# Folding token tiles on GpSimd ahead of a sum over all tokens, and a later, closer row of linear-attention steps

## The reference

```
xn = layernorm(x);  x = x + attention0(xn) + experts0(xn)     # softmax attention, top-2 experts
xn = layernorm(x);  x = x + attention1(xn) + experts1(xn)     # linear "flow" attention, top-4 experts
```

```
k_sum = k.sum(tokens);  sink_incoming   = 1 / sum((q + eps) * (k_sum + eps))
q_sum = q.sum(tokens);  source_outgoing = 1 / sum((k + eps) * (q_sum + eps))
k_so_sum = (k * source_outgoing).sum(tokens);  conserved_sink   = sum((q + eps) * (k_so_sum + eps)) + eps
q_si_sum = (q * sink_incoming).sum(tokens);    conserved_source = clip(sum((k + eps) * (q_si_sum + eps)) + eps, -1, 1)
out = ((q * sink_incoming) @ (k.T @ (v * softmax(conserved_source) * n))) * sigmoid(conserved_sink)
out = out @ proj_w.T + proj_b
```

## Time and profile before

| | us |
|---|---|
| median of 3 runs | 2818.09 |
| lowest and highest run | 2817.61, 2819.32 |
| the profiled execution | 2820.42 |
| its span | 2818.7 |
| PE busy | 2497.2 |
| DVE busy | 2185.9 |
| ACT busy | 1441.5 |
| POOL busy | 719.1 |

### The profile page before, as it was taken

One profiled execution on the slowest core, in us unless ns is written; L12 is line 12 of the kernel. 1 busy time (PEld: TensorE's weight loads), 2 busy tenths in 40 slices (PEclk: granted clock), 3 DMA queues, 4 the chain that ended last, 5 costly groups with the idle time before them and its releaser, 6 DMA issues.

```text
span 2818.7 us, 67301 instructions
## 1 busy us (share of the span) xinstructions
PE 2497.2 (89%) x26720; PEld 1807.0 (64%) x26720; DVE 2185.9 (78%) x3781; ACT 1441.5 (51%) x2616; POOL 719.1 (26%) x593
## 2 busy tenths in 40 slices
PE   4988989889898898988989889899898998989989
PEld 2766657675566665666667666576665766667656
DVE  4958878589786897777977779767797687985878
ACT  2746237563375534665246642566435573365723
POOL 1220342204322042220522215122151121520225
PEclk8999999999999999999999999999999999999999
DMA  6110211102111021110201112011120101201012
GB/s 224 39 37 4 87 49 39 38 2 98 38 39 38 2 102 35 39 38 25 82 31 42 35 39 75 24 46 31 47 71 26 44 27 54 68 27 47 19 63 65
DMA packets 93370, 136.25 MB, mean 48 GB/s; under 512 B 10111, under 2 KB 55240, under 8 KB 92552
## 3 DMA queue, kind: packets, MB, share of 16 engines
q1 hardware_dynamic: 84872, 115.16, 12.5%
q0 software_dynamic: 8192, 16.79, 2.0%
HBM read 101.31 MB, written 30.61 MB: 47 GB/s over the span
## 4 chain that ended last, share of the span: by engine, by line
PE 62%; DVE 19%; issue 11%; ACT 6%; POOL 2%; DVEq 0%; ACTq 0%; POOLq 0%
PE ps L1475 10%; PE ps L1343 8%; PE ps L1511 7%; PE ps L1417 6%; PE ps L1496 5%; DVE neg_max L1028 5%; PE ps L1548 4%; PE ps L1350 4%; PE ps L1439 3%; DVE probsT L1036 3%; ACT probs L701 2%; PE ps L1364 2%; PE ps L1317 2%; DVE ffn L1163 1%; PE ps L1428 1%
## 5 line engine op out<-in xcount | busy, mean ns | idle before, releaser
L1028 DVE TENSOR_REDUCE neg_max<-ps 128x1 f32<-128x1024 f32 x512 | 623.2, 1217 | 48.6 <-PE ps L1475 38.9
L701 ACT ACTIVATE probs<-ps,neg_max 128x1024 f32<-128x1024 f32 x512 | 571.6, 1117 | 156.3 <-DVE neg_max L1028 154.5
L1475 PE MATMUL ps<-keys,q_parts 64*128 64x512 f32 x3072 | 520.2, 445 | 82.8 <-ACT probs L701 57.0
L1343 PE MATMUL ps<-q_parts,w_split 128*128 128x512 f32 x1536 | 458.5, 435 | 42.6 <-DVE ffn L1146 24.0
L1496 PEld LDWEIGHTS ps<-ident,probs 64*128 64x128 f32 x8192 | 347.2, 143 | 96.4 <-ACT probs L701 17.3
L1343 PEld LDWEIGHTS ps<-q_parts,w_split 128*128 128x128 f32 x1536 | 284.7, 192 | 191.9 <-DVE ffn L1146 87.2
L1475 PEld LDWEIGHTS ps<-keys,q_parts 64*128 64x128 f32 x3072 | 264.1, 196 | 220.4 <-ACT probs L701 109.2
L600 POOL TENSOR_TENSOR probs<-ffn,q_parts 128x512 f32<-128x512 f32 x208 | 294.7, 1418 | 429.3 <-DVE ffn L1163 291.9
L757 ACT ACTIVATE ffn<-ffn 128x512 f32<-128x512 f32 x256 | 160.6, 630 | 468.8 <-DVE ffn L1146 468.4
L1036 DVE COPY probsT<-ps 128x512 f32<-128x512 f32 x512 | 348.6, 681 | 23.6 <-PE ps L1496 23.6
L1496 PE MATMUL ps<-ident,probs 64*128 64x64 f32 x8192 | 350.1, 227 | 16.4 <-ACT probsT L683 16.2
(11 more groups left out here) (213 smaller groups left out, 3297.0 us busy)
## 6 DMA issues: line engine op xcount, KB each, us to landing
w_split<-w_parts SPq DMA_DIRECT2D x132, 256.0 KB, 2.6
q_parts<-gate_rows SPq DMA_DIRECT2D x64, 512.0 KB, 4.0
y_rows<-probs SPq DMA_DIRECT2D x40, 256.0 KB, 2.2
x_in<-in_x SPq DMA_DIRECT2D x9, 512.0 KB, 4.3
w_parts<-q_parts SPq DMA_DIRECT2D x2, 2048.0 KB, 13.7
out<-x_mid SPq DMA_DIRECT2D x8, 512.0 KB, 3.2
ffn<-in_gate_up SPq DMA_DIRECT2D x1, 2048.0 KB, 8.9
probsT<-in_gate_up SPq DMA_DIRECT2D x1, 2048.0 KB, 13.1
```

The source lines that it names most:

```text
L701: nc.scalar.activation(probs[:, t % 3, :], banks(2 * (t % 2)), ACT.Exp, bias=neg_max[:, t % 4:t % 4 + 1], accum_out=row_sum[:, g % 2, t % ...
L1028: nc.vector.tensor_reduce(neg_max[:, t % 4:t % 4 + 1], banks(2 * (t % 2)), X, ALU.max, negate=True).then_inc(max_ready.sem, 1)
L1343: mm = nc.tensor.matmul(ps[:, bank, :], w_split[:, f % CHUNK_SLOTS, h, k * P:(k + 1) * P], tokens[:, half], start=(part == 0), stop=(part ...
L1475: mm = nc.tensor.matmul(ps[:, 2 * (t % 2) + c, :], q_parts[rows, j, q, n * P:(n + 1) * P], keys[rows, k, :], start=(part == 0), stop=(part ...
```

## The change

The sums over all tokens are made in two parts. POOL first adds token tiles 0 to 3 to tiles 4 to 7 (one instruction, 128x1024), and then the first two of these four to the other two (one instruction, 128x512). The two tiles that are left are summed by PE with two matmuls in place of eight. The tile `fold` takes the room of `v_comp`, which isn't in use at that point. `FLOW_HALVES` gives the units behind whose product POOL does the folds, 2 and 12. PE's sums wait for the fold (`folded`). All later steps of the linear attention get a higher unit number: the first sums move from unit 4 to 6, the second from 12 to 15, the values from 16 to 19, KV from 20 to 22, the output from 22 to 24, the heads from 25 to 26 and the projection from 28 to 29. The projection thus moves by one unit and the second sums by three, so that the steps between them stand closer together.

```diff
--- before.py
+++ after.py
@@ -51,7 +51,7 @@
 NORM_STATS = 8
 NORM_VAR = 13
 NORM_APPLY = 17
-NEXT_TRANSPOSE = 15
+NEXT_TRANSPOSE = 18
 
 
 H1, D1 = 16, 8
@@ -73,18 +73,19 @@
 
 FLOW_SIGMOID = 2
 SIGMOID_UNIT = 3
-FLOW_SUMS = 4
-
-FLOW_WEIGHTS = (4, 5, 6, 7, 8, 9)
+FLOW_SUMS = 6
+FLOW_HALVES = (2, 12)
+
+FLOW_WEIGHTS = (6, 7, 8, 9, 10, 11)
 FLOW_BIAS = 22
-FLOW_SUMS2 = 12
-FLOW_CONSERVED = (11, 12, 13, 14)
-FLOW_ALLOC = 15
-FLOW_VALUES = 16
-FLOW_KV = 20
-FLOW_OUT = 22
-FLOW_HEADS = 25
-FLOW_PROJ = 28
+FLOW_SUMS2 = 15
+FLOW_CONSERVED = (14, 15, 16, 17)
+FLOW_ALLOC = 18
+FLOW_VALUES = 19
+FLOW_KV = 22
+FLOW_OUT = 24
+FLOW_HEADS = 26
+FLOW_PROJ = 29
 
 DOWN_LAG = 4
 
@@ -197,6 +198,7 @@
         weighted = room[:, 3 * SEQ:5 * SEQ].rearrange("p (n c) -> p n c", n=NT)
         tmp = room[:, 5 * SEQ:6 * SEQ].rearrange("p (n c) -> p n c", n=NT)
         v_comp = room[:, 6 * SEQ:7 * SEQ].rearrange("p (n c) -> p n c", n=NT)
+        fold = room[:, 6 * SEQ:7 * SEQ].rearrange("p (n c) -> p n c", n=4)
 
         xT = [xT_first[:, :], room[:, 7 * SEQ:8 * SEQ]]
         q_normT = room[:, 7 * SEQ:8 * SEQ]
@@ -418,6 +420,7 @@
         sig_tanh = signal("sig_tanh", 1)
         qk_ready = signal("qk_ready", 1)
         sums_mm = signal("sums_mm", 2)
+        folded = signal("folded", 4)
         sums2_taken = signal("sums2_taken", 1)
         inv_flow_ready = signal("inv_flow_ready", 1)
         weighted_q = signal("weighted_q", 1)
@@ -601,6 +604,21 @@
                                             gate_bc[:, e % GATE_SLOTS, c * BANK:(c + 1) * BANK], ALU.mult
                                             ).then_inc(h_ready.sem, 1)
 
+                    if u in FLOW_HALVES:
+                        i = FLOW_HALVES.index(u)
+                        if i == 0:
+                            pool.wait_ge(qk_ready.sem, qk_ready.at(b, 1))
+                            x = qkv[:, :, 0:2 * D]
+                        else:
+
+                            pool.wait_ge(sums_mm.sem, sums_mm.at(b, 1))
+                            pool.wait_ge(weighted_q.sem, weighted_q.at(b, 1))
+                            pool.wait_ge(weighted_k.sem, weighted_k.at(b, 1))
+                            x = weighted
+                        nc.gpsimd.tensor_tensor(fold, x[:, 0:4, :], x[:, 4:8, :], ALU.add).then_inc(folded.sem, 1)
+                        pool.wait_ge(folded.sem, folded.at(b, 2 * i + 1))
+                        nc.gpsimd.tensor_tensor(fold[:, 0:2, :], fold[:, 0:2, :], fold[:, 2:4, :], ALU.add
+                                                ).then_inc(folded.sem, 1)
                     if u == FLOW_WEIGHTS[4]:
                         pool.wait_ge(inv_flow_ready.sem, inv_flow_ready.at(b, 1))
                         nc.gpsimd.tensor_tensor(heads(weighted[:, :, D:2 * D]), heads(flow_k),
@@ -1602,17 +1620,16 @@
                 def flow_step(u):
 
                     if u == FLOW_SUMS:
-                        pe.wait_ge(qk_ready.sem, qk_ready.at(b, 1))
-                        for n in range(NT):
-                            mm = nc.tensor.matmul(ps[:, 6, 0:2 * D], ones, qkv[:, n, 0:2 * D], start=(n == 0),
-                                                  stop=(n == NT - 1))
+                        pe.wait_ge(folded.sem, folded.at(b, 2))
+                        for n in range(2):
+                            mm = nc.tensor.matmul(ps[:, 6, 0:2 * D], ones, fold[:, n, :], start=(n == 0), stop=(n == 1))
                         mm.then_inc(sums_mm.sem, 1)
                     if u == FLOW_SUMS2:
                         pe.wait_ge(weighted_q.sem, weighted_q.at(b, 1))
                         pe.wait_ge(weighted_k.sem, weighted_k.at(b, 1))
-                        for n in range(NT):
-                            mm = nc.tensor.matmul(ps[:, 7, 0:2 * D], ones, weighted[:, n, :], start=(n == 0),
-                                                  stop=(n == NT - 1))
+                        pe.wait_ge(folded.sem, folded.at(b, 4))
+                        for n in range(2):
+                            mm = nc.tensor.matmul(ps[:, 7, 0:2 * D], ones, fold[:, n, :], start=(n == 0), stop=(n == 1))
                         mm.then_inc(sums_mm.sem, 1)
                     if u in (FLOW_SUMS2, FLOW_SUMS2 + 1):
                         c = u - FLOW_SUMS2
```

## The result

The changed kernel takes 2851.66 us (median of 4 runs, 2850.34 to 2855.58). In the same comparison the kernel before has 2817.85 us (4 runs, 2813.91 to 2819.32). The ratio is 1.0129, with a 95% interval from 1.0114 to 1.0144 (the quotient of the two medians is 1.0120). By the medians the change makes the kernel 34 us slower. The forecast was 2845 us, in a range from 2812 to 2856.

The account below looks back on a forecast made before the run. PE bounds units without a linear-attention step, DVE those with a weights or conserved step. Lost time of 3.6 us per sequence gives 8 x 3.6 = 29 us, taken as 27: 2818.1 + 27 = 2845 us, range 2812 to 2856.

Parts of the forecast that it names:

- PE's saved passes gain nothing: At both sums: 43 us less PE work over 8 sequences, the largest possible gain; at the second, DVE covers the saving.
- The fold's own price: On POOL, per sum: first add 2.35 us, second 1.28 us, about 3.7 us with its wait.
- DVE's products are held: Beside POOL's work: 2.1 us lost at the first fold, then about 1.1 and 0.1 us for units 4 and 5.
- sentence on two operands: A DVE instruction with two SBUF operands and a POOL instruction don't run together, so each fold stops the product beside it.
- The waits of PE: PE stalls 1.5 us at the first sums, 4 us at the second and 2.1 us before the KV matmuls.
- DVE's wait before the second sums: DVE waits 2.3 us before taking the second sums, whose inputs from the second fold are late.
- The sum: Per sequence the last down matmuls come 3.6 us later; 8 x 3.6 = 29 us, taken as 27 us.
- Its own signs: Short sums after 4 us idle; DVE idle 2 us; DVE products over 1.2 us; KV wait; POOL add 2.0 to 2.4.
- only a part of it: Rival, 20%: the wait before KV falls away or folds come between DVE's products; 1.5 us per sequence, 2830 us.
- Nothing in sum: Rival, 10%: folds and DVE's products run side by side; the stage ends within 0.1 us of before, 2818 us.
- Faster: Rival, 15%: DVE's product precedes the first fold, second fold ends before PE reaches the sums; 1.9 us won per sequence, 2803 us.
- Worse: Rival, 10%: POOL's delayed products meet DVE's in each unit, 0.5 us each over three more units; 2858 us.

Follow-up runs that it names:

- e9: Changed kernel with second sums and all steps behind them two units later, then KV, output and heads one more; 2814.61 us, ratio 0.9995.
- e11: Changed kernel without folds, eight matmuls for both sums, and KV, output, heads and projection one unit later; 2812.80 us, ratio 0.9984.
- e1: Changed kernel with its new unit numbers but no folds, both sums by eight matmuls on PE; 2825.73 us, ratio 1.0030.
- e5: Changed kernel with only the first fold, second sums by PE's eight matmuls again; 2824.66 us, ratio 1.0030.
- e4: Changed kernel with eight more matmuls on PE, result overwritten, ahead of its wait for the second fold; 2845.80 us (three runs), ratio 1.0100.
- e6: Changed kernel with only the second fold, first sums by PE's eight matmuls again; 2848.97 us, ratio 1.0105.
- e7: Changed kernel with the second sums and all steps behind them two units later, fold still behind unit 12; 2827.68 us, ratio 1.0033.
- e2: Against e1, POOL also does two folds of q and k tiles that nobody waits for or reads; 2840.69 us, ratio 1.0084.

## Why the prediction was right, step by step

- **PE's saved passes gain nothing: right.** The page shows 40.6 us less of PE (43 forecast), and e9 against e11 shows that of two folds 0.1 us per sequence reaches the end even where neither the second fold nor the values are waited for. From the sigmoid step to the first sums DVE has no idle time in the changed kernel, so its chain is the bound there.
- **The fold's own price: right.** 2.39 us for the first add where DVE didn't hold it (2.35 taken from the row of another one), 5.72 us from the sending of unit 12's product to the end of the second add (5.4 to 5.8 by the working).
- **DVE's products are held: right in place and size.** 2.80 - 0.68 = 2.1 us at the first fold, and 1.0 at the next product (1.1). The rows agree with what the prediction took from the Trainium skill (GPSIMD Engine Reference, 8. Key points): each of these products ends 0.55 us behind the POOL instruction that it met. But two SBUF operands are not the whole condition. The sigmoid step has one, keeps its 1.21 us, and POOL's product beside it takes 2.21 in place of 1.27. The prediction put such a row (996.57) under its sentence on two operands, which it doesn't fit. Also, e1 and e5 show that the holds at the first fold cost nothing in sum, since they take the place of the time that DVE otherwise waits for the eight matmuls. I had put the 3.5 us of lateness at the first sums under the heading of the fold. It is there in e1 without any fold (11.96 us), and belongs to the steps.
- **The waits of PE: right.** 1.3 us at the first sums (1.5 forecast), 3.96 at the second (4), 1.90 before KV (2.1). The rest from KV on is 25.96 us (25.9).
- **DVE's wait before the second sums: mis-sized.** 3.35 us in place of 2.3. Of the missing 1.05 us the slow clock in the sums themselves has 0.92 (2.05 - 1.13), and the same clock makes unit 16's matmuls late: 1.76 us more idle on DVE. I had costed the wait at its length alone and put the clock behind it at nothing. e4 puts the clock's part at 2.0 us in the third sequence and 1.6 on average.
- **The sum:** 3.6 us per sequence by the working, 5.2 measured in the stage (41.4 / 8). Some 1.4 us per sequence are missing outside the stage in the profiled execution, and 34 us in the medians are 4.2 per sequence. The forecast of 27 us was a fifth too small, by the term for the clock: the 1.6 us that the stage is over the working are what e4 gives back in it.
- **Its own signs:** of the five things it named three are there: short sums with 4 us of idle time before the second group, DVE products over 1.2 us beside each first add, and the wait before KV. Two are off in size, both at the second fold: DVE idles 3.35 us, not about 2, and the first add takes 2.80 us, outside 2.0 to 2.4. And the stretch from POOL's first product (992.73 before, 998.55 now) to the last group of down matmuls is 5.7 us longer, where the prediction called itself wrong outside 2.5 to 4.5. So the places and the order of the waits were right, and the size inside the stage was not. That the median, 2851.66 us, still lies just inside the forecast's own range of 2838 to 2852 is in part luck: the medians are 34 us apart, the stages of the profiles 41.
- **Shares:** of the 5.6 us of the third sequence, the closer KV step has 1.5 (e1), the first fold nothing (e5), and the second fold about 4 (e6), of which half is lateness and half the clock (e4).

Of the rivals, "only a part of it" failed at the KV wait, which was there. "Nothing in sum" failed at the held products. "Faster" named the condition that decides at the second sums, whether the second fold ends before PE is at the sums; e7 and e9 fulfil it, and then there is still no gain of the size it gave. Its other condition, that DVE's product goes ahead of the first fold, is fulfilled in no run: DVE's 3.3 us of waiting at the first sums are used up by the holds (e5). Whether they could be had with a first fold that holds nothing wasn't tried. "Worse" was half right in its mechanism. The backlog of POOL's products does meet DVE's (e2), once and not in three units.

## What to carry to other kernels

Work moved off the busiest engine pays only where that engine is the one waited for; look at the step that takes the result, and at what else holds that step. A sum moved to an idle but slow engine turns busy time into latency. It needs as many units of distance as the new chain is long (here 5.7 us; two more units than it was given were enough, one more wasn't tried), and each later step needs its old distance to its own releaser. An idle PE can cost more than the lateness of the result: count the slow clock behind it (here some 2 us on top of 2).

## What the runs showed of the hardware

- After 3.96 us without work PE ran at 1.2 GHz in all eight sequences, for some 5 us in six of them and some 3 us in two (four passes 2.05 us for 1.13, six 2.88 for 1.64), and with 3.62 us of otherwise useless matmuls in the wait it did not. Behind a wait of 1.9 us the clock fell in some sequences and not in others: in five of eight in e2, four in e7, one each in e1 and e4, and none in the changed kernel.
- The hold between POOL and DVE goes both ways. DVE products with two SBUF operands, sent while a POOL instruction ran, ended 0.55 us behind it: 2.80, 1.66 and 1.51 us in place of 0.68 (the adds and the product of POOL ended at 1006.94, 1009.84 and 1039.82). A second POOL instruction right behind the first, sent at 1007.02, did not make the hold longer. The other way round, a first add sent behind a DVE product took 2.80 us in place of 2.39.
- The second adds of 128x512 took 1.59 us, where POOL's product of that size takes 1.28. Each was sent about 0.5 us before the end of a held DVE product, so that a part may be a hold; no run has one that is undisturbed.
